# Feed-forward stage of a fused attention and FFN kernel: one-hot masks applied by VectorE from broadcast rows instead of by TensorE products

## What is computed

```python
x = x + xattn(layernorm(x), ctx, ctx, ...)
xt = layernorm(x)                                # then, in the FFN:
top1 = argmax(xt @ Wg.T, axis=-1)                # one of 8 experts per token
xhat = (xt - mean(xt)) * rsqrt(var(xt) + 1e-5)
for e in range(8):                               # H = 64 hidden units each
    h = gelu((xhat * s[e] + b[e]) @ W1[e] + b1[e])
    y = y + (top1 == e) * (h @ W2[e] + b2[e])
x = x + y
```

## Time and profile before

| | |
|---|---|
| median of 3 runs | 1468.85 us (1468.51 to 1470.84) |
| the profiled execution's own time | 1470.98 us |
| its span in the trace | 1468.8 us |
| PE busy | 1409.6 us (96%) |
| DVE, ACT, POOL busy | 1172.8, 866.1, 465.4 us |
| transfers | 190.89 MB, mean 130 GB/s |

### The profile page before, as it was taken

One profiled execution on the slowest core, in us unless ns is written; L12 is line 12 of the kernel. 1 busy time (PEld: TensorE's weight loads), 2 busy tenths in 40 slices (PEclk: granted clock), 3 DMA queues, 4 the chain that ended last, 5 costly groups with the idle time before them and its releaser, 6 DMA issues.

```text
span 1468.8 us, 39587 instructions
## 1 busy us (share of the span) xinstructions
PE 1409.6 (96%) x15438; PEld 1206.0 (82%) x15438; DVE 1172.8 (80%) x2880; ACT 866.1 (59%) x1451; POOL 465.4 (32%) x602
## 2 busy tenths in 40 slices
PE   6799999999999999999999999989999999999998
PEld 5688878888888888888888888867888888888887
DVE  4688888888888888888888888777777777777775
ACT  5466667777777777777777777753343333334342
POOL 4222322223223332323232323223333343433340
PEclk8899999999999999999999999999999999999999
DMA  7566755566556656665666566512222222221211
GB/s 187 119 161 174 178 154 147 158 167 177 154 162 172 179 143 174 171 178 145 169 174 168 146 167 172 156 32 87 72 73 73 73 73 73 72 73 64 81 59 43
DMA packets 150480, 190.89 MB, mean 130 GB/s; under 512 B 17631, under 2 KB 101146, under 8 KB 150298
## 3 DMA queue, kind: packets, MB, share of 16 engines
q1 hardware_dynamic: 150298, 188.38, 47.2%
HBM read 53.01 MB, written 33.55 MB: 59 GB/s over the span
## 4 chain that ended last, share of the span: by engine, by line
PE 73%; DVE 14%; issue 6%; ACT 6%; DMA 1%; POOL 0%; SPq 0%; ACTq 0%; DVEq 0%
PE st_ps L1235 13%; PE s_ps L1216 12%; PE pp_ps L1093 9%; DVE negmax L744 6%; PE s_ps L999 6%; PE pp_ps L1066 6%; PE st_ps L1027 6%; PE pv_ps L1041 5%; PE pp_ps L1101 4%; PE pv_ps L1049 3%; DVE cT_lo L770 3%; ACT xn L576 2%; PE s_ps L1223 2%; PE pp_ps L1182 2%; DVE negmax_wide L747 2%
## 5 line engine op out<-in xcount | busy, mean ns | idle before, releaser
L593 ACT ACTIVATE pT<-st_ps 128x1024 f32<-128x1024 f32 x256 | 263.1, 1028 | 130.3 <-PE st_ps L1027 130.3
L744 DVE TENSOR_REDUCE negmax<-s_ps 128x8 f32<-128x1024 f32 x256 | 311.3, 1216 | 29.1 <-PE s_ps L999 28.9
L1235 PE MATMUL st_ps<-w_hi,q_packed 128*128 128x256 f32 x1024 | 215.8, 296 | 0.2
L472 POOL TENSOR_TENSOR xb<-xin,bo_all 128x256 f32<-128x256 f32 x128 | 91.2, 734 | 273.8 <-DMA x_scratch<-xb 163.1
L1235 PEld LDWEIGHTS st_ps<-w_hi,q_packed 128*128 128x128 f32 x1024 | 167.8, 189 | 10.3 <-issue 6.0
L999 PE MATMUL s_ps<-k_packed,q_packed 96*128 96x128 bf16 x2048 | 157.9, 220 | 18.5 <-issue 8.3
L1216 PE MATMUL s_ps<-k_packed,w_hi 128*128 128x512 f32 x512 | 171.5, 423 | 0.6 <-ACT pT L647 0.6
L460 POOL TENSOR_TENSOR q_parts<-q,q_parts 128x1024 bf16<-128x1024 f32 x32 | 68.5, 2141 | 298.5 <-ACT q_parts L587 298.5
L1027 PE MATMUL st_ps<-q_packed,k_packed 98*128 98x128 bf16 x2048 | 158.4, 220 | 2.5 <-DMA q_packed<-negmaxT 2.4
L999 PEld LDWEIGHTS s_ps<-k_packed,q_packed 96*128 96x128 bf16 x2048 | 127.5, 98 | 39.4 <-DVE negmax L744 20.0
L636 ACT ACTIVATE offhotT<-pv_ps 96x512 bf16<-96x512 bf16 x31 | 18.4, 592 | 222.8 <-PE pv_ps L1203 222.8
(11 more groups left out here) (181 smaller groups left out, 3489.7 us busy)
## 6 DMA issues: line engine op xcount, KB each, us to landing
q_packed<-q_parts SPq DMA_DIRECT2D x192, 256.0 KB, 3.9
k_packed<-k_parts SPq DMA_DIRECT2D x192, 256.0 KB, 4.6
xin<-in_x_dram SPq DMA_DIRECT2D x32, 512.0 KB, 3.9
cin<-in_ctx_dram SPq DMA_DIRECT2D x32, 512.0 KB, 4.0
x_scratch<-xb SPq DMA_DIRECT2D x32, 512.0 KB, 4.6
xin<-x_scratch SPq DMA_DIRECT2D x32, 512.0 KB, 3.8
out_dram<-xb SPq DMA_DIRECT2D x32, 512.0 KB, 2.9
q_packed<-negmaxT SPq DMA_DIRECT2D x128, 8.0 KB
```

The lines of the kernel that those rows point to most:

```text
L472: last = g.tensor_tensor(xb[n % 2][:, b, :], xin[n % 2][:, b, :], bo_all[:], ALU.add)
L593: a.activation(pT[u % 2][:], st_ps[:], ACT.Exp, scale=DH ** -0.5).then_inc(s_exp, 1)
L744: v.tensor_reduce(own, s_ps[:].rearrange("p (h s) -> p h s", s=P), AX_X, ALU.max, negate=True).then_inc(s_red, 1)
L1235: t.matmul(o, h[n % 2][:, m, tok].bitcast(F32R), w[:, m, :].bitcast(F32R), start=(m == 0 and k == 0), stop=False)
```

## The change

1. **Masks.** From group 1 on there is no `mask` product and no `offhotT`. SP sends each of the eight rows of the kept one-hot tile `onehotT` (one expert's row: 512 bfloat16, 1 KB, in one partition) to 64 partitions of a mask tile. That is one transfer for each expert, and eight a group. VectorE multiplies each gelu block by its mask rows, in place (`mask_hidden`). The mask tiles lie in the attention's `q_parts` and `k_parts`, alternating by group. Two semaphores count the transfers, one for blocks 0 and 1, and one for blocks 2 and 3.
2. **Copies.** The high part of the hidden blocks is made by ScalarE (`hidden_hi`), after the mask. VectorE keeps the subtraction. ScalarE also normalises x (Identity with scale and bias), with a shift that GpSimd computes in two more steps.
3. **Order.** The logits and one-hot rows of group n+1 are made within group n, and x is normalised and transposed one group further ahead, so x2 has five buffers (two `xin`, `cin` and two halves of `v0`).
4. **Banks.** The outputs of four sequences have four PSUM banks, and the products go by hidden block first and sequence second, so that all of block 0 comes first.
5. Group 0 keeps the mask products and has a program of its own (`first_ffn_group` on ScalarE, VectorE and TensorE).

The core of the diff:

```diff
+        v_rows = v1[0][:].rearrange("p b h d -> p (b h d)").rearrange("p (k b d) -> p k b d", k=2, b=GB)
+        xf = [xin[0][:], xin[1][:], cin[:], v_rows[:, 0, :, :], v_rows[:, 1, :, :]]
+        XF = len(xf)
+        mask_rows = [part[:, 0:MC // C, :, :].rearrange("p a c t -> p (a c) t") for part in parts]
         onehotT = [sb(f"onehotT{n}", [3 * EP, GT], BF16) for n in range(2)]
-        offhotT = [sb(f"offhotT{n}", [3 * EP, GT], BF16) for n in range(2)]
+        offhotT = sb("offhotT", [3 * EP, GT], BF16)
...
-        f_ld = [sem(f"ffn_x2_loaded{n}") for n in range(2)]
+        f_ld = [sem(f"ffn_x2_loaded{n}") for n in range(XF)]
+        f_ml = [sem(f"ffn_mask_rows_loaded{n}") for n in range(2)]
+        f_hm, f_nm, f_sh = sem("ffn_hidden_masked"), sem("ffn_neg_mean"), sem("ffn_shift")
+        ML = 16 * EC * MC // 2
         f_st = [sem(f"ffn_out_stored{n}") for n in range(2)]
...
+
+        def o_ps(n, b):
+            if n > 0 and b >= 2:
+                return pp_ps[b - 2][:, 0:D]
+            return st_ps[:, b % 2 * 512:b % 2 * 512 + D]
...
+            def load_mask(n):
+                sp.wait_ge(f_oh, at(1, n, 1))
+                wait(sp, f_hm, at(MC, n - 3, MC))
+                for m in range(MC):
+                    for e in range(EC):
+                        row = EC * m + e
+                        sp.dma_start(mask_rows[n % 2][e * HID:(e + 1) * HID, m, :],
+                                     onehotT[n % 2][row:row + 1, :].unsqueeze(1).broadcast_to([1, HID, GT])
+                                     ).then_inc(f_ml[m // 2], 16)
+
             def group(n):
-                if n + 3 <= LAST:
-                    ffn_load(sp, n + 3)
+                if n + XF <= LAST:
+                    ffn_load(sp, n + XF)
+                if n < LAST:
+                    load_mask(n + 1)
                 store(n)
...
+                ffn_load(sp, n)
             for n in range(GROUPS):
                 group(n)
...
+                if n >= 2:
+                    g.tensor_tensor(neg_mean[:], mv[:, :, 0], neg_one[:], ALU.mult).then_inc(f_nm, 1)
+                    pool.wait_ge(f_r12, one)
+                    pool.wait_ge(f_nm, n - 1)
+                    g.tensor_tensor(shift[:], neg_mean[:], rstd[:], ALU.mult).then_inc(f_sh, 1)
...
             def keep_onehot(n):
                 act.wait_ge(f_ot, at(1, n, 1))
-                a.activation(offhotT[n % 2][:], onehotT_ps(n), ACT.Copy, bias=-1.0).then_inc(f_ote, 1)
+                a.activation(offhotT[:], onehotT_ps(n), ACT.Copy, bias=-1.0).then_inc(f_ote, 1)

             def keep_onehot_by_e(n):
+                act.wait_ge(f_ot, at(1, n, 1))
+                for loaded in f_ml:
+                    wait(act, loaded, ML * (n - 2))
                 a.copy(onehotT[n % 2][:], onehotT_ps(n)).then_inc(f_oh, 1)
...
+            def hidden_hi(n, m):
+                act.wait_ge(f_hm, at(MC, n - 1, m + 1))
+                a.copy(hT_hi[n % 2][:, m, :].bitcast(F32R), hidden32[m]).then_inc(f_hh, 1)
+
+            def ffn_normalise_by_shift(n):
+                act.wait_ge(f_sh, n - 1)
+                act.wait_ge(f_tr, at(C, n - 1, C))
+                for b in range(GB):
+                    a.activation(xn[:, b, :], xf[n % XF][:, b, :], ACT.Identity, bias=shift[:, b:b + 1],
+                                 scale=rstd[:, b:b + 1]).then_inc(f_xn, 1)
...
             def ffn_group(n):
-                if n > 0:
-                    keep_onehot(n)
                 gelu(n, 0)
+                hidden_hi(n, 0)
                 gelu(n, 1)
-                if n > 0:
-                    keep_onehot_by_e(n)
+                if n + 2 <= LAST:
+                    for c in range(C):
+                        keep_xT(n + 2, c)
+                hidden_hi(n, 1)
+                gelu(n, 2)
+                gelu(n, 3)
+                hidden_hi(n, 2)
                 if n < LAST:
-                    for c in range(C):
-                        keep_xT(n + 1, c)
-                for m in range(2, MC):
-                    gelu(n, m)
+                    keep_onehot_by_e(n + 1)
+                hidden_hi(n, 3)
                 if n < LAST:
-                    if n == 0:
-                        act.wait_ge(st_x2[1], 8 * GROUPS)
                     copy(n + 1)
-
-            for n in range(GROUPS):
+                if n + 3 <= LAST:
+                    ffn_normalise_by_shift(n + 3)
+
...
+            def mask_hidden(n, m):
+                dve.wait_ge(f_he, at(MC, n, m + 1))
+                dve.wait_ge(f_ml[m // 2], ML * n)
+                v.tensor_tensor(hidden32[m], hidden32[m], mask_rows[n % 2][:, m, :], ALU.mult).then_inc(f_hm, 1)
+
+            def hidden_hi(n, m):
+                dve.wait_ge(f_he, at(MC, n, m + 1))
+                v.tensor_copy(hT_hi[n % 2][:, m, :].bitcast(F32R), hidden32[m]).then_inc(f_hh, 1)
+
+            def hidden_lo(n, m):
+                dve.wait_ge(f_hh, at(MC, n, m + 1))
+                v.tensor_tensor(hT_lo[n % 2][:, m, :].bitcast(F32R), hidden32[m], hT_hi[n % 2][:, m, :],
+                                ALU.subtract).then_inc(f_hl, 1)
...
             def ffn_group(n):
                 more = n < LAST
-                if 0 < n < LAST:
-                    ffn_normalise(dve, n + 1)
-                if 0 < n <= LAST - 2:
-                    ffn_stats_of(dve, n + 2)
-                for m in range(MC):
-                    split_hidden(n, m)
-                if n == 0:
-                    ffn_stats_of(dve, 2)
-                add(n, 0)
+                if n + 3 <= LAST:
+                    ffn_stats_of(dve, n + 3)
+                mask_hidden(n, 0)
+                if more:
+                    keep_logits(n + 1)
+                hidden_lo(n, 0)
+                mask_hidden(n, 1)
+                if more:
+                    route(n + 1)
+                hidden_lo(n, 1)
+                mask_hidden(n, 2)
+                mask_hidden(n, 3)
+                hidden_lo(n, 2)
+                hidden_lo(n, 3)
                 if more:
                     split_xT(n + 1)
-                add(n, 1)
-                if more:
-                    keep_logits(n + 1)
-                add(n, 2)
-                if more:
-                    route(n + 1)
-                add(n, 3)
-
-            for n in range(GROUPS):
+                for b in range(GB):
+                    add(n, b)
+
...
                         pe.wait_ge(f_xl, at(C, n, C))
                     for c in range(C):
-                        t.matmul(h_ps[m % 2], w[:, c, e, :].bitcast(F32R), x[n % 2][:, c, :].bitcast(F32R),
-                                 start=(k == 0 and c == 0), stop=False)
-
-            def mask(n, m):
+                        mm = t.matmul(h_ps[m % 2], w[:, c, e, :].bitcast(F32R), x[n % 2][:, c, :].bitcast(F32R),
+                                      start=(k == 0 and c == 0), stop=(n > 0 and k == 2 and c == C - 1))
+                if n > 0:
+                    mm.then_inc(f_h, 1)
+
...
+            def output(n, b, m):
+                o = o_ps(n, b)
                 tok = slice(b * T, (b + 1) * T)
-                if parts[0] == 0:
-                    wait(pe, f_out, at(GB, n, b - 1))
-                for m in parts:
-                    if b == 0:
-                        pe.wait_ge(f_hl, at(MC, n, m + 1))
-                    for k, (h, w) in enumerate(((hT_hi, w2_hi), (hT_hi, w2_lo), (hT_lo, w2_hi))):
-                        t.matmul(o, h[n % 2][:, m, tok].bitcast(F32R), w[:, m, :].bitcast(F32R),
-                                 start=(m == 0 and k == 0), stop=False)
-                if parts[-1] == MC - 1:
+                if m == 0:
+                    if n == 0:
+                        wait(pe, f_out, b - 1)
+                    else:
+                        pe.wait_ge(f_out, at(GB, n - 1, b + 1 if n > 1 or b > 1 else b + 3))
+                    if n > 0 and b >= 2 and n + 2 <= LAST:
+                        pe.wait_ge(f_tre, at(C, n + 2, b - 1))
+                if b == 0:
+                    pe.wait_ge(f_hl, at(MC, n, m + 1))
+                for k, (h, w) in enumerate(((hT_hi, w2_hi), (hT_hi, w2_lo), (hT_lo, w2_hi))):
+                    t.matmul(o, h[n % 2][:, m, tok].bitcast(F32R), w[:, m, :].bitcast(F32R),
...
+            def outputs(n, batches, m):
+                for b in batches:
+                    output(n, b, m)
+
...
             def ffn_group(n):
                 more = n < LAST
-                if n > 0:
-                    hidden(n, 0)
-                    turn_onehot(n)
-                    hidden(n, 1)
-                    mask(n, 0)
-                    mask(n, 1)
-                if 0 < n < LAST:
-                    for c in range(C):
-                        turn(n + 1, c)
-                for m in range(2, MC):
-                    hidden(n, m)
-                    mask(n, m)
-                for parts in (range(MC - 1), range(MC - 1, MC)):
-                    for b in range(2):
```

(28 more changed lines are left out.)

106 lines of the change are left out of this document (81 added, 25 removed).

## The result

| | before | changed |
|---|---|---|
| median of the runs | 1468.97 us | 1681.52 us (1679.67 to 1686.3) |
| span in the trace | 1468.8 us | 1681.3 us |
| ratio to before | | 1.145 (1.1425 to 1.1474) |

The changed kernel is 212.5 us slower. The forecast was 1714 us, with a range of 1640 to 1830.

A forecast was written before the change was run, and what follows sets the result against it. TensorE bounds the old kernel at 14.83 us a group; mask transfers would bound the changed one: 22.7 - 14.83 = 7.9 us for 31 groups, +245 on 1470.98 is 1716, less 2.1 for the median: 1714 us, range 1640 to 1830.

The forecast's parts named there:

- The mechanism: FFN groups with masks: VectorE waits for serial mask transfers, two groups' loads cannot overlap, 7.9 us more a group; chance 81%.
- The rate: Mask transfers from one row: 27 GB/s, 2.43 us each and 19.4 for eight; range 22.8 to 30 GB/s.
- The length of a group: FFN group: eight transfers 19.4, latency 1.2, mask product, copies and handovers; 22.7 us taken, against 14.83 before.
- The tail: After the transfers land: mask product 0.69, high-part copy 0.60, one-hot copy 0.58, three handovers about 0.1 each.
- The second limit: DMA engines in a group: masks 19.4, store 1.7 and load about 1.8 add up to 22.9 us.
- TensorE's need: TensorE's work in an FFN group: 14.83 - 1.20 = 13.6 us, without masks and with new banks and order.
- four banks take away 0.19: Output products of the third sequence in a group: 1.61 - 1.42 = 0.19 us saved, no longer waiting for their bank.
- rival 1: FFN masks arrive in time at 0.2 us a transfer, a group lasts 13.6 us, kernel 1432 us; chance 11%.
- SP's issues: SP issues a mask transfer in about 0.6 us, well ahead of the transfers themselves.
- What was to be seen: Signs in the FFN trace: period 22 to 24 us, TensorE 60 to 65%, VectorE waiting some 5 us twice a group.
- rival 3: Row at 13 GB/s, kernel some 2330 us, chance 3%; smaller version: TensorE's clock falls, group about 25 us, 1780.
- Rival 2: Mask transfers: one row serves several engines better, 43 GB/s gives 1490 us, partial overlap 1480 to 1640; chance 5%.

The follow-up runs named there:

- experiment 1: Changed kernel with mask transfers sent for groups 1 and 2 only, later groups multiplying by what lies in the mask tiles: 1451.66 us, ratio 0.988.
- experiment 2: Changed kernel with the one-hot rows stored to DRAM and spread from there by four loads of 128 KB: 1439.49 us, ratio 0.980.
- experiment 4: Changed kernel with each mask transfer carrying only 256 of its 512 tokens from group 3 on: 1451.63 us, ratio 0.988.
- experiment 5: Changed kernel with each mask transfer reading two copies of its row, 32 partitions each: copies 32 apart 1753.94 us, 64 apart 1493.55 us.
- experiment 6: Changed kernel with every second one-row transfer reading a copy of its row further on: 64 partitions 1458.86 us, 32 partitions 1682.2 us.
- experiment 7: Changed kernel with a ninth mask transfer per group into an unread tile: from row 0 1692.7 us, from row 7 1759.94 us.
- experiment 3: Changed kernel with the masks made by the old TensorE product in every group and no mask transfers: 1464.16 us, ratio 0.997.

## Why the prediction was right, point by point

- **The mechanism: right.** VectorE waits for the mask transfers, these run nearly one behind the other (rows 3 and 4 excepted), and two groups' loads can't overlap. Experiments 1, 2 and 4 each take the transfers' time away in another manner, and each is faster than before.
- **The rate: right, and for a reason the prediction did not have.** Chosen were 27 GB/s, with 2.43 us for a transfer; the trace has 28 GB/s and 2.36 us. The step from the 25 GB/s of the earlier trace rows to 27 had no ground there: its 6.6% is already more than one engine in sixteen (6.25%), so that engine left no gaps for others to fill. On that ground alone it is luck that the choice came so near. The prediction took the limit to be the single row. Runs 5 to 7 show that it is an outlet that several partitions share: rows 4 and 7 share it and rows 0 and 7 don't, 32 partitions further is the same, 64 further another. The Trainium skill, "SBUF — State Buffer", section on Door 1, gives this map (0 to 3 with 32 to 35, 4 to 7, 64 to 67 each on one port) and 27.2 GB/s for a port. All four relations that the runs show agree with it.
- **The length of a group: 22.7 forecast, 21.80 measured (21.67 on average).** Eight transfers with latency were 19.4 + 1.2 = 20.6 and are 19.85. With 2.34 us each, at the measured 28 GB/s, the same sum gives 18.7 + 1.2 = 19.9, but that it fits so well is partly luck, for the landings in experiment 7 show two things that it leaves out, and they nearly offset each other. The first transfer lands 4.6 us after its issue, and not 2.36 + 1.2 = 3.6; the second and third are 1.0 us late too. Why was not settled (in experiment 6, where the second transfer reads another outlet, the first lands after 3.7). And the fourth and fifth come 1.3 us sooner than one behind the other, since rows 3 and 4 have different outlets. The tail was 2.2 with the handovers and is 1.95. (The terms listed add up to 22.8, not to the 22.6 written; the 22.7 used stands between that and the second limit.) The second limit, 22.9 us for the masks plus a store and a load on the same engines, did not hold. From 1322.5 to 1326.2 us the DMA moved 137 to 277 GB/s. The store and the load filled the engines beside the last mask packets, and their time does not add to that of a full outlet. In all a group is 22.7 - 21.67 = 1.0 us shorter on average than forecast, 32 of the 32.5 us between 1714 and 1681.5.
- **TensorE's need: the term that was mis-sized.** 14.83 - 1.20 = 13.6 was forecast; it is 13.81. Right were the mask products (14.70 - 13.81 = 0.89 against 0.91) and roughly the order (0.13 against 0.1). Wrong was "four banks take away 0.19", as the row behind the gate in experiment 3 shows. That did not touch the forecast, since TensorE is not on the path, but rival 1's 1432 us should have been about 1437: with masks in time the kernel takes 1439.5.
- **SP's issues: wrong, without a price here.** Issues were to take 0.6 us each and be far ahead. They do so for three, and then take 2.36 us each. The store and the load behind them are issued 12.5 and 15 us late, and the store lands after 8.7 us where the earlier trace rows had 2.9. Five x2 buffers hide that.
- **What was to be seen.** A period of 22 to 24 us: 21.8. Waits of some 5 us twice a group: 5.3 and 3.8 in the group from 1306. The engines nearly always busy at 35 to 60 GB/s: 77% at 68 GB/s. By the prediction's own numbers it should have been 69, masks, store and load together, 3 x 0.52 MB in 22.7 us. TensorE at 60 to 65%: 73%, since its granted clock fell to 0.87 and its products took longer (a hidden product 474 ns on average; 414 with two-row copies 64 apart, at the full clock). It is the small version of rival 3, a lower mean clock where TensorE has gaps, and it cost next to nothing, since no product stands in the chain above.
- **Rival 1** (masks in time) was wrong for the transfers as the change has them, and near in what it said of the rest (1432 against 1439.5 us). **Rival 2** (one row serves several engines better than one) is refuted: sixteen engines get 28 GB/s out of one row. Its other form, transfers from different rows that overlap in part, does occur, but in the changed kernel only where rows 3 and 4 meet.

## What to carry to other kernels

In these runs the rate of a transfer out of one or two partitions went by the separate outlets that they reach. A broadcast out of one partition, or out of neighbours in turn, gets one outlet, 28 GB/s with sixteen engines and 25 with two. Before masks or rows are moved from TensorE to a broadcast transfer, divide the bytes that leave each outlet by that rate and compare with the time of a group. If it doesn't fit, send the few source rows to DRAM first and broadcast from there, or read copies that lie 64 partitions apart in turn: here a group went from 21.8 us to 13.8 and 14.5.

## What the runs showed of the hardware that was not expected

- Two transfers in flight that read different outlets did overlap. Eight one-row transfers took about 12.2 us with sources 64 apart in turn, and 19.85 without. The Trainium skill, "SBUF — State Buffer", section "Can I just issue two DMAs to hit both halves?", says that two concurrent transfers, on tiles at partitions 0 and 64, came to only 6% more than one. For transfers that read a single row each, these runs show otherwise, and the measurement decides.
- SP's issue blocks. With about four such transfers outstanding each further issue took as long as a transfer (2.36 us), also for the store and the load behind them.
- An engine by itself moved some 24 GB/s (47 for two, experiment 5), so with one-row sources an outlet was used up by little more than one engine, and the other fifteen added waiting: in the changed kernel they are 80% busy for 28 GB/s.
- Products that stand right behind the gate's small ones took 0.19 us longer than elsewhere, whatever they were: 1.61 against 1.42 in the earlier trace rows, 1.60 against 1.41 in the kernel of experiment 2, and 1.60 in that of experiment 3. Why is open.
